# Reordering the head of a fused GroupNorm, CondConv and sign-convolution kernel

## The chip, the cores and the metric

The kernel runs on one core of a Trainium2 chip. The metric is the time on the device in microseconds (us); the median of several runs counts. Engines are named as the profile names them: PE is TensorE, DVE is VectorE, ACT is ScalarE, POOL is GpSimd, SP is SyncE, which here only issues DMAs.

## What is computed

The input is x, 16 images of 128 channels of 32 x 32, in float32. Reference, cut:

```python
def gn(v):    # 32 groups of 4 channels, over the group's channels and pixels
    return (v - mean_g(v)) / sqrt(var_g(v) + 1e-5)

def cond(x, w_route, b_route, w_experts, bn...):
    routing = sigmoid(mean_hw(x) @ w_route.T + b_route)         # 4 experts
    y = conv3x3(x, w_experts)                                   # (B, E, 128, 32, 32)
    out = einsum("beohw,be->bohw", y, routing)
    return silu(out * inv + (bn_beta - bn_mean * inv))

x = x + cond(gn(x))
x = x + conv3x3(gn(x), sign(W))
```

The sum over experts is done on the weights: for each image the four expert kernels are mixed by its routing into one 3 x 3 kernel.

## The kernel before

Channels lie on the 128 partitions, one image is 1,024 columns. Each image goes through the same steps:

- the statistics of the input (`nm` mean, `var` variance), by DVE with `bn_stats` for image 0 (`half_stats`, `aggregate`), by ACT with two passes over the image for the others (`mean_in`, `var_in`);
- a chain of small operations, numbered c. PE sums the means over each group (`group_means`), ACT squares the deviations (`deviations`), PE sums the variances (`group_vars`), DVE takes them over (`variance`), POOL raises them to -0.5 (`power`, `rstd`), DVE makes `nbias`, `zr` and `pooled` (`biases`, `pool_routes`), PE sums `pooled` over the channels (`route_logits`), ACT makes `route` (`routing`). All results of PE in it lie in one PSUM bank, `ps`;
- ACT normalises the image into `xn` (`normalise`) and weighs the first expert into `U` (`mix`), DVE adds the other three (`mix(i, e)`; row by row for image 0, `mix_row`);
- the first convolution. Image 0 is done directly, in six parts (`direct_part(0, n, half)`: three kernel rows n, two halves), from `xn` and `U` into bank pair `pd`. Images 1 to 15 use Winograd's form along the rows: DVE transforms `xn` into `V` (`transform_sums`, `transform`) and `U` into `UM` (`even_rows`, `kernel_rows`), PE multiplies (`minus_points`, `plus_points`, `end_points`, into `pb`, `pa`, `pe_`), ACT copies `pb` (`copy_minus`), DVE inverts into `y` (`inverse_inner`, `inverse_outer`);
- ACT applies silu, and the result is added to the image in `X` (`residual`, by DVE for images 0, 14 and 15, by a DMA with addition from POOL's queue for the others);
- the statistics of the sum go with chain c = i + 3 (`mean_mid`, `var_mid`), which also serves the input of image i + 3. ACT normalises the sum to `hi` (float16) and `hn`, DVE takes their difference `lo` (`low_part`), PE convolves `hi` and `lo` with the signs of W (`sign_half`, line 425) into the bank pair `pc`, ACT copies it out (`evacuate`) and a DMA adds it to the stored sum.

Each engine has an order written out by hand, and counting semaphores tie them. In pass t of the main loop PE does the points of image t, then the sign convolution of image t - 1; DVE mixes for image t + 1, inverts image t, makes `lo` of t - 1 and transforms image t + 2. Ahead of the loop is the head, which the change is about. There PE does `WARM[0]` = 9 products of ones, after a wait for the parameters (`prm_loaded`), then chain 0 with `route_logits(0)`, `WARM[1]` = 8 more, then the six direct parts with chains 1 and 2 strung between them (lines 456 to 476). A float32 product is two instructions in the trace. The groups before DVE's main loop are at lines 881 to 913, ACT's at 626 to 651, the loads of SP at 272 to 284. SP issues the two halves of image 0, the parameters, weight row G1, image 1, weight rows G0 and G2, images 2 and 3, and the signs' weights.

Of the kernel before, what the change touches and what calls it, by code (L numbers as in the profile page):

```python
# [45 lines left out]
WARM = (9, 8)  # L46
# [4 lines left out]
def build(nc, x, w_experts, w_sign, params, out):  # L51
# [6 lines left out]
    with ExitStack() as ctx:  # L58
# [45 lines left out]
        halves = sb("halves", [C, 2, 6])  # L104
        agg = {i: sb(f"agg{i}", [C, 2]) for i in (0, B - 1)}
# [21 lines left out]
        gnm = ps[:, 0:2 * CHAINS].rearrange("p (c k) -> p c k", k=2)  # L127
        gvar = ps[:, 64:64 + 2 * CHAINS].rearrange("p (c k) -> p c k", k=2)
        logits = ps[:, 128:128 + E * B].rearrange("p (i e) -> p i e", e=E)
# [91 lines left out]

        def dma_added_before(i):

            return sum(1 for j in range(i % 2, i, 2) if j not in DVE_RESIDUAL)
# [40 lines left out]
        def _(sp):  # L265
# [72 lines left out]
        def _(pe):  # L338
# [6 lines left out]
            def group_means(c):  # L345
# [9 lines left out]
                mm_(gnm[:, c, a:b], gmat[:], nm[:, c, a:b], start=True, stop=True).then_inc(gnm_ready, 1)  # L355

            def group_vars(c):
# [6 lines left out]
                mm_(gvar[:, c, a:b], gmat[:], var[:, c, a:b], start=True, stop=False)  # L364
                mm_(gvar[:, c, a:b], gmat_hw[:], dev2[:, c, a:b], start=False, stop=True).then_inc(gvar_ready, 1)  # L365

            def route_logits(i):
                pe.wait_ge(pooled_ready, i + 1)
                mm_(logits[:, i, :], ones[:], pooled[:, i, :], start=True, stop=True).then_inc(logits_ready, 1)  # L369
# [87 lines left out]
            pe.wait_ge(prm_loaded, 16)  # L457
# [50 lines left out]
        def _(act):  # L508
# [28 lines left out]
            def deviations(c):  # L537
                a, b = cols(c)
                act.wait_ge(gnm_ready, c + 1)
                for k in range(a, b):  # L540
                    activation(dev2[:, c, k:k + 1], gnm[:, c, k:k + 1], ACT.Square, bias=nm[:, c, k:k + 1],
                               scale=-1.0).then_inc(dev2_ready, 1)

            def normalise(i):
# [5 lines left out]
                activation(xn[i % 2][:, 1:1 + H, :], img(i).rearrange("p (h w) -> p h w", h=H), ACT.Identity,  # L550
# [128 lines left out]
        def _(dve):  # L679
# [234 lines left out]
            for t in range(1, B + 1):  # L914

                c = t + LAG - 1
                if t > 1:
                    mix(t + 1, 1)
# [63 lines left out]
```

## Time and profile before

| | |
|---|---|
| median of 3 runs | 303.5 us (302.35 to 303.65) |
| profiled execution, its own time | 302.17 us |
| its span, first to last instruction | 300.3 us |
| mean granted clock of PE | 0.983 |
| PE busy | 278.8 us (93%) |
| DVE busy | 254.9 us (85%) |
| ACT busy | 188.8 us (63%) |
| POOL busy | 42.8 us (14%) |

The profile is of one execution. Its time is 1.9 us more than its span, for what lies before the first and after the last instruction, and 1.3 us less than the median. A timeline row gives the start, the duration (of a group: from its first start to its last end), the engine and line, what is written from what, the count, and in brackets the idle time before it with what ended it. Ends overlap with the next start by up to some 0.1 us, so costs are best read from start to start.

### The profile page before, as it was taken

The numbers are of one execution on the slowest core, as the hardware profiler recorded it, in microseconds if no ns is written. First come the engines' busy times: TensorE is split into PE (matmuls) and PEld (weight loads), VectorE is DVE, ScalarE is ACT, GpSimd is POOL, SyncE is SP. The second block draws the span as 40 slices with busy tenths as digits, with TensorE's granted clock in tenths as the row PEclk, the third lists the DMA queues.
The fourth block names the chain that finished last, engine by engine and source line by source line (L and its number), as shares of the span: only waits on it lengthen the run. The fifth ranks groups of instructions, "written<-read, shape, count | busy, mean of one in ns | idle before, by whom it ended". The sixth has DMA issues, their size and how long they took to land.

```text
span 300.3 us, 3929 instructions
## 1 busy us (share of the span) xinstructions
PE 278.8 (93%) x1350; PEld 193.8 (65%) x1350; DVE 254.9 (85%) x487; ACT 188.8 (63%) x300; POOL 42.8 (14%) x56
## 2 busy tenths in 40 slices
PE   3799692699999999999999999999999999999896
PEld 3754381367685859585867677676858595858454
DVE  3238989789999999999999999999999999960932
ACT  1446370768778687769595968687786874644230
POOL 2001200102121212121211202021212121201000
PEclk9999979699999999999999999999999999999999
DMA  7999410054544453626263544545453436230411
GB/s 244 396 383 323 168 72 0 1 140 72 140 70 113 70 100 93 119 80 120 83 104 105 82 131 70 142 70 141 71 123 67 91 86 127 79 63 0 70 72 70
DMA packets 10963, 34.14 MB, mean 114 GB/s; under 512 B 1216, under 2 KB 3008, under 8 KB 10944
## 3 DMA queue, kind: packets, MB, share of 16 engines
q0 software_dynamic: 3888, 14.16, 28.0%
q1 hardware_dynamic: 7056, 19.74, 17.4%
q8 instruction: 11, 0.18, 0.2%
q14 instruction: 8, 0.07, 0.1%
HBM read 11.34 MB, written 15.73 MB: 90 GB/s over the span
## 4 chain that ended last, share of the span: by engine, by line
PE 83%; DVE 11%; ACT 2%; issue 1%; DMA 1%; POOL 0%; SPq 0%; DVEq 0%; ACTq 0%
PE pc L425 40%; PE pa L390 12%; PE pb L390 12%; PE pe_ L390 11%; DVE U L764 3%; PE pd L343 3%; PE pd L380 2%; PE ps L365 1%; DMA prm<-params 1%; PE ps L364 1%; DVE e_rows L796 1%; PE ps L355 1%; PE ps L369 1%; PE pb L425 1%; DVE U L754 1%
## 5 line engine op out<-in xcount | busy, mean ns | idle before, releaser
L425 PE MATMUL pc<-lo,ws 128*128 128x496 f16 (+5 forms) x288 | 64.7, 372 | 0.0
L764 DVE SCALAR_TENSOR_TENSOR U<-we,route,U 128x1152 f32<-128x1152 f32 x45 | 63.8, 1417 | 1.0
L425 PE MATMUL pc<-hi,ws 128*128 128x496 f16 (+5 forms) x288 | 63.9, 377 | 0.4 <-ACT hi L610 0.4
L425 PEld LDWEIGHTS pc<-hi,ws 128*128 128x128 f16 x288 | 28.5, 102 | 30.9 <-issue 2.2
L425 PEld LDWEIGHTS pc<-lo,ws 128*128 128x128 f16 x288 | 28.2, 102 | 28.2 <-DVE lo L872 0.3
L390 PE MATMUL pa<-V,UM 128*128 128x256 f32 (+1 forms) x180 | 42.0, 383 | 0.0
L390 PE MATMUL pb<-V,UM 128*128 128x256 f32 (+1 forms) x180 | 42.0, 384 | 0.0
L305 POOL TENSOR_TENSOR rstd<-ve,nhalf 128x2 f32<-128x2 f32 (+1 forms) x19 | 17.2, 905 | 168.1 <-DVE ve L728 168.1
L390 PE MATMUL pe_<-V,U 128*128 128x256 f32 (+1 forms) x180 | 40.6, 375 | 0.0
L390 PEld LDWEIGHTS pb<-V,UM 128*128 128x128 f32 x180 | 34.9, 194 | 5.2
L390 PEld LDWEIGHTS pe_<-V,U 128*128 128x128 f32 x180 | 34.1, 190 | 3.8
L390 PEld LDWEIGHTS pa<-V,UM 128*128 128x128 f32 x180 | 33.3, 192 | 3.3
L610 ACT ACTIVATE hi<-X,nbias,rstd 128x1024 f16<-128x1024 f32 (+2 forms) x17 | 20.1, 1190 | 17.9 <-DVE nbias L734 17.9
L534 ACT ACTIVATE junk_mid<-X,nm 128x1024 f32<-128x1024 f32 x15 | 17.2, 1148 | 17.6 <-DMA X<-y 16.7
L550 ACT ACTIVATE xn<-X,nbias,rstd 128x1024 f32<-128x1024 f32 x16 | 19.7, 1229 | 11.3 <-DVE nbias L734 11.3
L584 ACT ACTIVATE minus<-pb 128x512 f32<-128x512 f32 x15 | 8.9, 596 | 27.7 <-PE pb L390 27.7
L872 DVE TENSOR_TENSOR lo<-hn,hi 128x1024 f16<-128x1024 f32 x16 | 19.5, 1217 | 3.2 <-ACT hn L617 3.2
L595 ACT ACTIVATE y<-y,bn_shift,bn_tiles 128x1024 f32<-128x1024 f32 x14 | 17.4, 1240 | 6.3 <-DVE y L847 6.3
L309 POOL DMA_DIRECT2D X<-y x13 | 11.5, 884 | 65.8 <-ACT y L595 65.8
L728 DVE TENSOR_SCALAR ve<-ps 128x2 f32<-128x2 f32 (+1 forms) x19 | 2.9, 153 | 20.6 <-PE ps L365 20.6
L617 ACT ACTIVATE hn<-X,nbias,rstd 128x1024 f32<-128x1024 f32 x16 | 19.6, 1227 | 0.0
L796 DVE SCALAR_TENSOR_TENSOR e_rows<-xn 128x1024 f32<-128x1024 f32 x15 | 18.3, 1220 | 0.9 <-ACT xn L550 0.9
(85 smaller groups left out, 389.0 us busy)
## 6 DMA issues: line engine op xcount, KB each, us to landing
X<-x SPq DMA_DIRECT2D x15, 512.0 KB, 5.2
out<-X SPq DMA_DIRECT2D x14, 512.0 KB, 2.6
out<-ev POOLq DMA_DIRECT2D x14, 512.0 KB, 5.4
X<-y POOLq DMA_DIRECT2D x13, 512.0 KB, 4.5
we<-w_experts SPq DMA_DIRECT2D x3, 768.0 KB, 7.3
out<-X SPq DMA_DIRECT2D x3, 256.0 KB, 2.0
ws_raw<-w_sign SPq DMA_DIRECT2D x1, 576.0 KB, 10.8
X<-x SPq DMA_DIRECT2D x2, 256.0 KB, 2.8
```

The costliest lines, as they stand in the source:

```text
L305: g.tensor_tensor(rstd[:, c, a:b], ve[:, c, a:b], nhalf[:, a:b], ALU.pow).then_inc(rstd_ready, 1)
L309: g.dma_start(img(i), flat3(y[i % 2][:]), accum_op=ALU.add).then_inc(added[i % 2], 16)
L390: mm = mm_(bank[:, :, j, c0:c1], weights[:, kx * C:(kx + 1) * C], V[t % 2][:, :, k, c0 + kx - 1:c1 + kx - 1], start=(n == 0), stop=(n == K ...
L425: mm = mm_(rows[:, r0 - first // W:r1 - first // W, c0:c1], ws[:, tap * C:(tap + 1) * C], (hi, lo)[part][i % 2][:, r0 + ky - 1:r1 + ky - 1 ...
L534: activation(junk["mid"][:], img(i), ACT.Square, bias=nm[:, c, MID:MID + 1], scale=1.0 / ROOT_HW, accum_out=var[:, c, MID:MID + 1]).then_i ...
L550: activation(xn[i % 2][:, 1:1 + H, :], img(i).rearrange("p (h w) -> p h w", h=H), ACT.Identity, bias=nbias[:, i, IN:IN + 1], scale=rstd[:, ...
L595: activation(flat3(y[i % 2][:]), flat3(y[i % 2][:]), ACT.Silu, bias=bn_shift[:, 0:1], scale=bn_tiles[:, 0:1], accum_out=ysum[:, i:i + 1]). ...
L610: activation(hi[i % 2][:, first:last, :], img(i).rearrange("p (h w) -> p h w", h=H)[:, first:last, :], ACT.Identity, bias=nbias[:, c, MID: ...
L617: activation(hn[:], img(i), ACT.Identity, bias=nbias[:, c, MID:MID + 1], scale=rstd[:, c, MID:MID + 1]).then_inc(hn_ready, 1)
L764: v.scalar_tensor_tensor(out=flat(U[i % 2][:]), in0=flat(we[:, e, :, :]), scalar=route[:, i, e:e + 1], in1=flat(U[i % 2][:]), op0=ALU.mult ...
L796: v.scalar_tensor_tensor(out=flat3(e_rows[:]), in0=flat(xn[i % 2][:, 0:H, :]), scalar=-4.0, in1=flat(xn[i % 2][:, 2:2 + H, :]), op0=ALU.mu ...
L872: v.tensor_tensor(flat(lo[i % 2][:]), hn[:], flat(hi[i % 2][:]), ALU.subtract).then_inc(lo_ready, 1)
```

## The change

- Loads: image 1 is issued right behind the parameters, ahead of weight row G1.
- PE: the warm products don't wait for the parameters any more; 4 instead of 8 products after the first chains. Chains 0 and 1 run side by side before the direct parts, chain 2 between them. Chains 1 and 2 write to the banks of `pc` (`small_bank`), so that `group_means` of 1 and 2 waits for nothing of the chain before.
- DVE: the statistics of image 1 by `bn_stats`, ahead of `variance(0)`; chain 1 ahead of the mixing of image 0; in the head `variance(2)`, `biases(2)`, `pool_routes(2)` one step later or earlier among the mixes of image 1, and `residual(0)` behind the transform of image 2.
- DVE, pass 1: `variance(3)`, the inverse of image 1 and the biases first, then the mixes 2 and 3 of image 2 with `low_part(0)` between them, then its even and kernel rows. The two first operations of `inverse_inner` are a function of their own, `inverse_sums`.
- ACT: image 0 is normalised in two parts (17 and 15 rows), the first weighted row G1 between them; the first product of PE waits for the first part alone. `sign_weights`, `routing(2)` and `var_in(3)` go ahead of `silu(0)`, `copy_minus(1)` ahead of `var_mid(0)`.
- Passes from 2 on keep their order.

```diff
-WARM = (9, 8)
+WARM = (9, 4)
...
+        def small_bank(c):
+            return pc[:, c - 1, :] if c in (1, 2) else ps[:]
...
             sp.dma_start(prm[:], params).then_inc(prm_loaded, 16)
+            load(1)
             load_row(G1, 1)
-            load(1)
...
-                wait(pe, nbias_ready, c)
-                wait(pe, zr_ready, min(c, B))
-                wait(pe, th_ready, min(c, B))
+                if c > 2:
+                    last = 1 if c == 3 else c
+                    pe.wait_ge(nbias_ready, last)
+                    pe.wait_ge(zr_ready, min(last, B))
+                    pe.wait_ge(th_ready, min(last, B))
...
-                pe.wait_ge(xn_ready, i + 1)
+                pe.wait_ge(xn_ready, 1 if i == n == half == 0 else i + 2)
...
             pe.wait_ge(zeroed, 2)
-            pe.wait_ge(prm_loaded, 16)
             warm(WARM[0])
             pe.wait_ge(gmat_ready, 2)
             group_means(0)
             group_vars(0)
+            group_means(1)
+            group_vars(1)
             route_logits(0)
+            route_logits(1)
             warm(WARM[1])
-
             direct_part(0, 0, 0)
-            group_means(1)
             direct_part(0, 0, 1)
-            group_vars(1)
             direct_part(0, 1, 0)
-            route_logits(1)
+            group_means(2)
             direct_part(0, 1, 1)
-            group_means(2)
+            group_vars(2)
             direct_part(0, 2, 0)
-            group_vars(2)
+            route_logits(2)
             direct_part(0, 2, 1)
-            route_logits(2)
...
             act.wait_ge(nm_in_ready, 1)
             deviations(0)
-            normalise(0)
+            act.wait_ge(nm_in_ready, 2)
+            deviations(1)
+            act.wait_ge(nbias_ready, 1)
+            normalise_rows(0, 0, H // 2 + 1)
             routing(0)
-            mix(0)
-            mean_in(1)
-            var_in(1)
-            deviations(1)
+            mix_first_row(0, G1)
+            normalise_rows(0, H // 2 + 1, H)
+            mix_first_row(0, G0)
+            mix_first_row(0, G2)
+            routing(1)
+            normalise(1)
+            mix(1)
             mean_in(2)
-            normalise(1)
-            routing(1)
-            mix(1)
             var_in(2)
             deviations(2)
             mean_in(3)
+            sign_weights()
             normalise(2)
-            sign_weights()
+            routing(2)
+            var_in(3)
             silu(0)
             mean_mid(0)
-            routing(2)
             mix(2)
-            var_mid(0)
-            var_in(3)
             for t in range(1, B):
-                if t > 1:
+                if t == 1:
+                    copy_minus(t)
                     var_mid(t - 1)
                     deviations(t + LAG - 1)
-                copy_minus(t)
-                if t == 1:
+                else:
+                    var_mid(t - 1)
                     deviations(t + LAG - 1)
+                    copy_minus(t)
...
             aggregate(0, 0, IN, nm_in_ready, var_in_ready)
             parameters()
+            dve.wait_ge(x_loaded[1], 16)
+            half_stats(1, 0)
+            half_stats(1, 1)
+            aggregate(1, 1, IN, nm_in_ready, var_in_ready)
             variance(0)
             dve.wait_ge(route_prm_ready, 2)
             biases(0)
             pool_routes(0)
+            variance(1)
+            biases(1)
+            pool_routes(1)
             batch_norm()
             mix_row(0, 0)
             mix_row(0, 1)
-            variance(1)
             mix_row(0, 2)
-            biases(1)
-            pool_routes(1)
             transform_sums(1)
             transform(1)
             mix(1, 1)
+            variance(2)
             mix(1, 2)
-            variance(2)
+            biases(2)
+            pool_routes(2)
             mix(1, 3)
             even_rows(1)
-            biases(2)
             kernel_rows(1, -1)
-            pool_routes(2)
             kernel_rows(1, 1)
-            residual(0)
             transform_sums(2)
             transform(2)
+            residual(0)
             mix(2, 1)
...
                 if t == 1:
+                    variance(c)
+                    inverse_sums(t)
+                    biases(c)
+                    pool_routes(c)
+                    inverse_inner(t)
+                    inverse_outer(t)
+                    mix(t + 1, 2)
+                    low_part(t - 1)
+                    mix(t + 1, 3)
+                    even_rows(t + 1)
                     kernel_rows(t + 1, -1)
                     kernel_rows(t + 1, 1)
-                    inverse_inner(t)
-                    variance(c)
-                    inverse_outer(t)
-                    biases(c)
-                    pool_routes(c)
```

## Rows read from the trace of the kernel before

**Rows 1.** Waits over the whole run: engine, line, waited for, total, times, longest us.

```profile
PE ps L369 <- DVE pooled L744: 12.0, 3, 7.8
...
DVE ve L728 <- PE ps L365: 20.6, 5, 7.2
```

**Rows 2.** Busy time of each engine in one steady pass, with clock and DMA.

```profile
72.80:88.75 15.95, 15.95 (x83) 11.26 (x82) 15.67 (x30) 11.99 (x19) 2.74 (x3) 1.00 0.47 99
```

**Rows 3.** Timeline of PE: start, duration, line, operation, count, idle before.

```profile
4.58 4.18 PE L343 MATMUL pd<-ones 128*128 128x128 f32 x18 [4.58 <-DMA prm<-params]
8.55 0.42 PE L355 MATMUL ps<-nm,gmat 128*128 128x1 f32 x2
...
16.03 3.30 PE L380 MATMUL pd<-xn,U 128*128 128x512 f32 x6
...
19.30 2.77 PE L380 MATMUL pd<-xn,U 128*128 128x512 f32 x6
...
30.90 2.61 PE L380 MATMUL pd<-xn,U 128*128 128x480 f32 x6
...
36.45 4.14 PE L390 MATMUL pb<-V,UM 128*128 128x256 f32 x12
...
55.58 5.25 PE L425 MATMUL pc<-hi,ws 128*128 128x512 f16 x18 [0.39 <-ACT hi L610]
...
72.80 3.97 PE L425 MATMUL pc<-hi,ws 128*128 128x512 f16 x18
```

**Rows 4.** Timeline of DVE, same columns.

```profile
3.44 1.40 DVE L714 BATCH_NORM_STATS2 halves<-X 128x6 f32<-128x512 f32 x2 [1.25 <-DMA X<-x]
...
10.53 0.16 DVE L728 TENSOR_SCALAR ve<-ps 128x1 f32<-128x1 f32 x1 [5.00 <-PE ps L365]
...
11.75 0.22 DVE L744 SCALAR_TENSOR_TENSOR pooled<-wroute,zr,bshare 128x4 f32<-128x4 f32 x1
...
13.84 3.76 DVE L754 SCALAR_TENSOR_TENSOR U<-we,route,U 128x384 f32<-128x384 f32 x6 [1.41 <-ACT U L564]
...
29.50 2.87 DVE L764 SCALAR_TENSOR_TENSOR U<-we,route,U 128x1152 f32<-128x1152 f32 x2
...
73.61 1.22 DVE L872 TENSOR_TENSOR lo<-hn,hi 128x1024 f16<-128x1024 f32 x1
```

**Rows 5.** Waits of DVE between 13.8 and 73.7 us.

```profile
DVE ve L728 <- PE ps L365: 5.7, 2, 4.8
DVE lo L872 <- ACT hn L617: 2.1, 1, 2.1
DVE X L853 <- ACT y L591: 1.4, 1, 1.4
...
DVE e_rows L796 <- ACT xn L550: 0.9, 1, 0.9
```

**Rows 6.** Third large load; then landing times of X and of the weight rows.

```profile
2.12 0.43 SPq L270 DMA_DIRECT2D we<-w_experts  x1
...
DMA to landing us min/median/max: 2.7/4.8/9.9
...
DMA to landing us min/median/max: 5.0/7.3/9.0
```

**Rows 7.** Busy time and clock, one microsecond after the pause of PE.

```profile
38.00:39.00 1.00, 1.00 (x4) 0.82 (x3) 0.49 (x1) 0.94 (x5) 0.00 (x0) 0.50 0.00 0
```

**Rows 8.** POOL: the power of chain 2, and all powers of the page.

```profile
32.52 1.71 POOL L305 TENSOR_TENSOR rstd<-ve,nhalf 128x1 f32<-128x1 f32 x1 [8.98 <-DVE ve L728]
...
L305 POOL TENSOR_TENSOR rstd<-ve,nhalf 128x2 f32<-128x2 f32 (+1 forms) x19 | 17.2, 905 | 168.1 <-DVE ve L728 168.1
```

**Rows 9.** Timeline of ScalarE (ACT), same columns as Rows 3.

```profile
34.99 1.24 ACT L550 ACTIVATE xn<-X,nbias,rstd 128x1024 f32<-128x1024 f32 x1 [5.31 <-DVE nbias L734]
...
43.03 0.39 ACT L541 ACTIVATE dev<-ps,nm 128x1 f32<-128x1 f32 x2
...
83.29 0.60 ACT L584 ACTIVATE minus<-pb 128x512 f32<-128x512 f32 x1 [1.84 <-PE pb L390]
```

More of the change, by code:

```diff
@@ L220, in cols, with gnm, gvar, logits @@
             return (IN if c < LAG else MID), (2 if c < B else 1)
+        def small_bank(c):
+            return pc[:, c - 1, :] if c in (1, 2) else ps[:]
+        def gnm(c, a, b):
+            return small_bank(c)[:, 2 * c + a:2 * c + b]
+        def gvar(c, a, b):
+            return small_bank(c)[:, 64 + 2 * c + a:64 + 2 * c + b]
+        def logits(c):
+            return small_bank(c)[:, 128 + E * c:128 + E * (c + 1)]
         def dma_added_before(i):
@@ L350, in group_means @@
                     pe.wait_ge(nm_mid_ready, c - LAG + 1)
[L352 to L355 removed]
+                if c > 2:
[3 more added lines that the diff above has]
+                    pe.wait_ge(th_ready, min(last, B))
+                mm_(gnm(c, a, b), gmat[:], nm[:, c, a:b], start=True, stop=True).then_inc(gnm_ready, 1)
             def group_vars(c):
@@ L363, in group_vars @@
                 pe.wait_ge(dev2_ready, dev2s(c))
-                mm_(gvar[:, c, a:b], gmat[:], var[:, c, a:b], start=True, stop=False)
-                mm_(gvar[:, c, a:b], gmat_hw[:], dev2[:, c, a:b], start=False, stop=True).then_inc(gvar_ready, 1)
+                mm_(gvar(c, a, b), gmat[:], var[:, c, a:b], start=True, stop=False)
+                mm_(gvar(c, a, b), gmat_hw[:], dev2[:, c, a:b], start=False, stop=True).then_inc(gvar_ready, 1)
             def route_logits(i):
                 pe.wait_ge(pooled_ready, i + 1)
-                mm_(logits[:, i, :], ones[:], pooled[:, i, :], start=True, stop=True).then_inc(logits_ready, 1)
+                mm_(logits(i), ones[:], pooled[:, i, :], start=True, stop=True).then_inc(logits_ready, 1)
             def direct_part(i, n, half):
                 slot, ky = ((G1, 1), (G0, 0), (G2, 2))[n]
-                pe.wait_ge(xn_ready, i + 1)
+                pe.wait_ge(xn_ready, 1 if i == n == half == 0 else i + 2)
                 pe.wait_ge(mixed, mixes_before(i) + (E - 1) * (n + 1))
@@ L549, in normalise, with normalise_rows @@
                     act.wait_ge(direct_ready, 2 * (i - 1))
-                activation(xn[i % 2][:, 1:1 + H, :], img(i).rearrange("p (h w) -> p h w", h=H), ACT.Identity,
+                normalise_rows(i, 0, H)
+            def normalise_rows(i, first, last):
+                activation(xn[i % 2][:, 1 + first:1 + last, :],
+                           img(i).rearrange("p (h w) -> p h w", h=H)[:, first:last, :], ACT.Identity,
                            bias=nbias[:, i, IN:IN + 1], scale=rstd[:, i, IN:IN + 1]).then_inc(xn_ready, 1)
@@ L560, in mix @@
                 act.wait_ge(route_ready, i + 1)
-                if i < ND:
-                    for g in (G1, G0, G2):
-                        act.wait_ge(we_loaded[g], 16)
-                        activation(U[i % 2][:, g, :], we[:, 0, g, :], ACT.Copy,
-                                   scale=route[:, i, 0:1]).then_inc(mix_first, 1)
-                    return
                 if i - 2 >= ND:
@@ L574, in mix, with mix_first_row @@
                            scale=route[:, i, 0:1]).then_inc(mix_first, 1)
+            def mix_first_row(i, g):
+                act.wait_ge(route_ready, i + 1)
+                act.wait_ge(we_loaded[g], 16)
+                activation(U[i % 2][:, g, :], we[:, 0, g, :], ACT.Copy, scale=route[:, i, 0:1]).then_inc(mix_first, 1)
             def sign_weights():
@@ L935, in _ @@
                     kernel_rows(t + 1, 1)
+                    inverse_sums(t)
                     inverse_inner(t)
                     inverse_outer(t)
-                elif t == B - 1:
-                    variance(c)
-                    biases(c)
-                    inverse_inner(t)
-                    inverse_outer(t)
-                if t < B:
                     low_part(t - 1)
```

44 lines of the change are left out of this document (21 added, 23 removed).

## The prediction, made before the changed kernel was run

> **What bounds the kernel now.** I read first the waits of TensorE (PE) over the whole run, then busy time in stretches of the steady part, then the timelines of the head, engine by engine. The waits say where PE is not the bound: 12.0 us behind `pooled`, in three waits, the longest 7.8 us [rows 1]; all three lie before 55 us. From the first sign convolution at 55.58 on, PE is busy to the end but for 1.2 us in the tail. In the stretches one image costs PE 15.95 us of 15.95, at full clock, and VectorE (DVE) 15.67 us of the same 15.95 [rows 2]. The DVE rest of 0.28 is in small gaps, so DVE's own pass is hardly shorter than PE's. Two consequences. Whatever time PE's steady part starts earlier, the end comes earlier by the same, if DVE comes along. And DVE hardly catches up: what it is late at the second image it is late until the last images, where it has nothing left to mix (a single wait of 7.2 us there [rows 1]). The question is therefore where DVE and PE stand when image 1 is reached: DVE's `low_part(1)`, before at 73.61 [rows 4], and PE's convolution of image 1, before at 72.80 [rows 3].
>
> **The new start, step by step.** PE's warm products no longer wait for the parameters. Before they began at 4.58 and the group means of image 0 stood behind them until 8.55 [rows 3]. Now they begin at about 1.0 (the ones are filled by then), last the same 3.97, and end at 5.0, before the statistics of image 0, which DVE has at 5.3. So the means go at 5.35, and `variance(0)` could be fed 10.53 - 8.55 = 1.98 later, at 7.3 [rows 3, 4].
>
> It isn't, because DVE now has the statistics of image 1 ahead of it. Image 1 now takes the place of the first weight row, issued at 2.12. Loads of X land 2.7 to 9.9 us after issue, median 4.8; the weight row in that place is the quickest of the three, 5.0 us [rows 6]. Image 1 is 256 KB smaller, 0.65 us at the 400 GB/s of this stretch, so I take 4.3 us: it lands at 6.4 (ends 4.8 and 12.0). Its statistics last as image 0's, which began at 3.44 [rows 4] and ended at 5.3, 1.85 us: until 8.3. Then `variance(0)` at 8.3 instead of 10.53, `pooled(0)` 1.44 later as before, at 9.75. Chain 1 runs in banks of its own: means at 8.35, `variance(1)` 1.98 later at 10.35, `pooled(1)` ready 1.44 later at 11.8, and `batch_norm` ends at 12.3. ScalarE has the first image's route at 11.3 and, with half an image normalised instead of a whole one, the first weighted row at 11.9; the weights, now behind image 1, land at 8.5 at the latest by the sum above and are hidden. So DVE starts mixing at 12.3 instead of 13.84 [rows 4]: gain 1.5. Three mixes of 0.63 (3.76 for six) end at 14.2. PE has its second logits until 12.3 and then 8 warm passes instead of 16, 1.8 us at the 0.22 of the first 18, so it ends at 14.1 and hides behind the mixes. The first product starts at s = 14.3 instead of 16.03: gain 1.7.
>
> **The clock.** The first direct part takes 3.30 us where its twins take 2.77 [rows 3]: so half rate held until about 17, though the clock column doesn't record it. After the later pause the column does: 0.50 at 38 to 39 [rows 7]. Nothing in the change makes PE busier before 14.3 than it was, so I let it rise at the same 17: 2.7 us at half rate, of which 1.35 is lost, where 0.5 was. c = 1.3, with the ends 0.3 (it rises as early after the first activity as the earlier start allows) and 3.0.
>
> **Image 0 and the fill.** The wait of PE on DVE goes over to DVE waiting on PE. DVE does the three mixed rows, the transform of image 1 and its first mix without a stop. That is the time from 13.84 to 30.95, the middle of the two mixes at 29.50, less the idle 4.8 and 0.9 and the 0.5 of chain 1 that is now done before [rows 4, 5]: 10.8 us, so until 23.1. The wait of 4.8 is gone, but `variance(2)` stands next, and PE reaches the variances of image 2 only after four direct parts. These are s + c + 10.9 = 26.5 (14.87 from 16.03 to 30.90, less 0.5 for the clock, one part of 2.77 and small ones [rows 3]): DVE idles 3.4 us here. This is the largest new wait; behind it are the mixes 2 and 3 of image 1 and with them PE's first minus points.
>
> The `rstd` of chain 2 took 1.71 us beside mixes of 1.42 us [rows 8]; with one mix between it and its use, DVE waits 0.45 more. By the Trainium skill ("SBUF — State Buffer", section "SBUF: two separate sides") the port pair that VectorE and GpSimd share is locked for a whole instruction, so the power would wait out the mix and then take its own time; the row agrees, and by that rule nothing more is lost at `variance(3)`, where the operations behind it read one operand from PSUM.
>
> From `variance(2)` at 26.5: mix 1.5, wait and biases 0.9, mix 1.45, even rows 0.95, kernel rows 1.9: the last kernel row for PE's minus points is ready at 32.3 and PE ends the direct parts at s + c + 16.0 = 31.6. So the minus points start at 31.9 instead of 36.45 [rows 3], without the pause of 2.7 us and, I take it, without the fall of the clock that cost 1.4 of their 4.14 us. DVE goes on with the transform of image 2, the residual and a mix until 39.5. ScalarE has from the end of the direct parts on what it had between 34.99 and 43.4 [rows 9], less the signs of the weights (1.05, now in an idle piece) and plus 0.4 for the residual it waits for: 8.0 us, until 39.7. So PE has the variances of image 3 at 40.2 and `variance(3)` is at 40.25: DVE idles 0.75. Before it waited 2.1 for `hn` and 0.9 for `variance(4)` [rows 5]; neither is left, for ScalarE gets its biases at 41.7, `hi(0)` is there at 42.9, and the first convolution starts at 43.0 instead of 55.58, 12.5 us earlier.
>
> That is not the gain, for DVE still owes its work. From 13.84 to 73.61 it had 59.77 us, of which 5.7 + 2.1 + 1.4 + 0.9 = 10.1 were idle [rows 5]: 49.6 of work, 49.1 without chain 1. The reordering in pass 1 (inverse before the mixes of image 2) changes none of it. So `low_part(1)` is at 12.3 + 49.1 + 3.4 + 0.45 + 0.75 = 66.0; adding the same operations one by one I get 65.7. I take 65.8: DVE gains 7.8.
>
> **What PE gains over DVE.** In the steady part PE may stand earlier against DVE than it did. Three links hold it. `lo` is ready 1.15 + 0.1 after `low_part` starts, and is wanted 3.8 after the convolution starts (18 products, 3.97 with their overlap [rows 3]): 73.61 + 1.25 against 72.80 + 3.8, room 1.75. `hi` comes one ScalarE pass behind `nbias`, long before `low_part`, and has more room. The residual's DMA and the statistics of the sum end 1.84 before the minus points that ScalarE then waits for [rows 9]: room 1.65. The smallest decides, so PE's convolution of image 1 is at 65.8 - 0.81 - 1.65 = 63.3; by the `hi` link alone it could start at 62.4. Before it PE idles 2.6 us with only the logits in it, about the pause (36.45 less 33.5, the end of the direct parts) after which the clock fell, and with a fall it counts as 63.8. I take 63.5, gain 9.3. From there on it is the old order at 15.95 a pass, and the tail has room for DVE's 1.5 us of lag.
>
> **The sum.** 72.8 - 63.5 = 9.3 us. The profiled run lasted 302.17 us, with a span of 300.3; it would become 292.9. It is 1.3 us under the median of the three runs, 303.5, so the forecast for a median is 294.2.
>
> **Rivals.** First, nothing over DVE: the DMA of the residual or the fall of the clock takes the 1.5 us by which PE moves up, gain 7.8, 295.7 us; against it, the 1.84 us of room in a steady pass. Chance 0.2. Second, the clock stays at half rate for most of the direct parts (c = 3), or image 1 lands a microsecond or two later than I take: each late microsecond goes through `variance(0)` to everything; gain 6 to 7.5, 296 to 297.5. For it: the head loads fully use the DMA. Chance 0.15. Third, the change doesn't do what it says: the first chain and the pauses of PE in pass 1 stay, because ScalarE's queue (silu, minus copy, then the residual statistics) is late, and only the 1.7 of the start and a clock fall of 1.4 are saved: 300.4. ScalarE's 8.0 us beside DVE's 7.9 speak against. Chance 0.06. Fourth, slower: DVE is the bound of every pass once PE has moved up, and its pass is longer than 15.95. The place is `nbias` behind `rstd`: where the power waits out a mix it took 1.71 where the mean of all is 0.9 [rows 8], 0.8 more a pass, over 13 passes 10.4 us against the 9.3 gained: 304.6. It decides from 0.7 us a pass. Against it, in passes after the first the operations beside the power are the same short ones. Chance 0.03. Fifth, better: the clock rises early (c = 0.3) or image 1 lands 2.7 after issue, the quickest of all, so that the chain of image 0 runs by its own inputs, at 7.3: 1.0 each, gain 10.3 to 11, 292.8. Chance 0.14. My forecast, 293.3 to 295.2, has 0.42.
>
> **How the numbers follow.** The low end takes in the fifth case and a median that lies only 0.3 over the profiled run, as two runs of before allow: 291.3. The high end takes in the first two cases: 298.0. What a measurement of this kernel can tell from no change is about 0.5%, 1.5 us. Only the third and fourth case and mishaps reach there: faster 0.93, same 0.04, slower 0.03.
>
> **What would show it.** Right: PE's first product at 14.3, DVE idle about 3.4 us before `variance(2)` near 26.5 and under 1 us before `variance(3)` near 40, minus points of image 1 at 31.9, the first convolution near 43, PE idle about 2.6 us before the convolution of image 1 at 62.4 to 64, passes of 15.95 after it. Wrong: a pass of more than 16.0 (fourth), a wait of PE for `dev` or `lo` in every pass (first), a first product later than 15 or direct parts of 5 us (second), or a pause over 4 us before the first convolution (third).

## The result, and the profile after

| | before | after |
|---|---|---|
| median | 303.28 us (302.35 to 303.65, 4 runs) | 293.07 us (292.71 to 293.47, 4 runs) |
| profiled execution, its own time | 302.17 us | 292.85 us |
| its span | 300.3 us | 291.0 us |
| PE busy | 278.8 us (93%) | 276.5 us (95%) |
| DVE busy | 254.9 us (85%) | 255.8 us (88%) |
| ACT busy | 188.8 us (63%) | 185.6 us (64%) |

The ratio of the times is 0.967, with the interval 0.965 to 0.970. The median before is of four runs here, the profiled one among them. The span is shorter by 300.3 - 291.0 = 9.3 us. Of these, PE's idle time gives 7.0 (21.5 before, 14.5 after). PE's busy time fell by 2.3, for the minus points of image 1 and the first sign convolution no longer run at the lower clock, as the rows below show.

The timeline of PE after, in the columns of [rows 3]:

```profile
1.03 4.21 PE L353 MATMUL pd<-ones 128*128 128x128 f32 x18 [1.03 <-POOL ones L327]
5.43 0.56 PE L367 MATMUL ps<-nm,gmat 128*128 128x1 f32 x2 [0.19 <-DVE nm L738]
...
14.00 8.72 PE L392 MATMUL pd<-xn,U 128*128 128x512 f32 x18
...
28.60 2.61 PE L392 MATMUL pd<-xn,U 128*128 128x480 f32 x6
31.31 2.78 PE L402 MATMUL pb<-V,UM 128*128 128x256 f32 x12
...
42.68 3.97 PE L437 MATMUL pc<-hi,ws 128*128 128x512 f16 x18
...
61.09 0.39 PE L381 MATMUL ps<-pooled,ones 128*128 128x4 f32 x2 [1.84 <-DVE pooled L761]
61.98 3.98 PE L437 MATMUL pc<-hi,ws 128*128 128x512 f16 x18 [0.51 <-ACT hi L623]
66.36 2.08 PE L437 MATMUL pc<-lo,ws 128*128 128x512 f16 x9 [0.40 <-DVE lo L892]
69.11 0.39 PE L367 MATMUL ps<-nm,gmat 128*128 128x2 f32 x2 [0.66 <-ACT junk_mean L524]
...
79.45 3.97 PE L437 MATMUL pc<-hi,ws 128*128 128x512 f16 x18
```

Against [rows 3], the warm products start at 1.03 instead of 4.58, the first direct product at 14.00 instead of 16.03, the minus points of image 1 at 31.31 instead of 36.45 and at full rate (2.78 us, not 4.14), the first sign convolution at 42.68 instead of 55.58 and at full rate (3.97, not 5.25). Ahead of image 1's convolution PE idles 1.84 + 0.51 us, and there the clock did not fall: 3.98 us. Behind it stand two small waits, 0.40 for `lo` and 0.66 for ACT's `junk_mean`, the image mean. The pass before has one of them, 0.33 for `junk_mean` at 48.88; from 79.45 on the passes are the old ones. Counted back from there, image 1's convolution stands at 79.45 - 15.95 = 63.50, where it was at 72.80: the 9.3 us of the span.

The timeline of DVE after, same columns:

```profile
6.59 1.29 DVE L731 BATCH_NORM_STATS2 halves<-X 128x6 f32<-128x512 f32 x2 [1.04 <-DMA X<-x]
8.29 0.15 DVE L745 TENSOR_SCALAR ve<-ps 128x1 f32<-128x1 f32 x1
...
10.20 0.16 DVE L745 TENSOR_SCALAR ve<-pc 128x1 f32<-128x1 f32 x1 [0.48 <-PE pc L377]
...
11.94 5.60 DVE L771 SCALAR_TENSOR_TENSOR U<-we,route,U 128x384 f32<-128x384 f32 x9
...
25.84 0.16 DVE L745 TENSOR_SCALAR ve<-pc 128x1 f32<-128x1 f32 x1 [3.30 <-PE pc L377]
...
27.76 0.16 DVE L751 SCALAR_TENSOR_TENSOR nbias<-pc,rstd 128x1 f32<-128x1 f32 x1 [0.44 <-POOL rstd L315]
...
39.83 0.16 DVE L745 TENSOR_SCALAR ve<-ps 128x2 f32<-128x2 f32 x1 [1.00 <-PE ps L377]
...
65.10 1.21 DVE L892 TENSOR_TENSOR lo<-hn,hi 128x1024 f16<-128x1024 f32 x1
...
81.03 1.21 DVE L892 TENSOR_TENSOR lo<-hn,hi 128x1024 f16<-128x1024 f32 x1
```

Image 1 is in at 6.59. The new wait of DVE is 3.30 us before `variance(2)`, and it is the largest one left before the tail. `low_part(1)` is at 65.10 instead of 73.61 [rows 4], so DVE gained 8.5 us, and the next follows 15.93 later.

Busy time after, in a steady pass and in two microseconds of the head (columns: stretch, its length, busy time of PE, weight loads, DVE, ACT, POOL with counts, granted clock, DMA share, GB/s):

```profile
15.00:16.00 1.00, 1.00 (x3) 0.48 (x2) 0.96 (x3) 1.00 (x2) 0.00 (x0) 0.50 1.03 413
16.00:17.00 1.00, 1.00 (x4) 0.53 (x3) 0.93 (x3) 1.00 (x2) 0.00 (x0) 0.92 1.02 401
...
78.95:94.90 15.95, 15.95 (x82) 11.21 (x81) 15.67 (x30) 11.89 (x21) 2.66 (x3) 1.00 0.48 100
```

The steady pass is that of [rows 2]: 15.95 us, DVE busy for 15.67. In the head the clock was at the lower of its two levels, 1.2 GHz, until about 16.2, while PE already worked on the direct parts.

### The profile page after: what moved, and what is told of

Read it like the earlier page. It is cut to its first block, busy times and chain, and to the rows that moved or that the text cites. A ratio compares the mean times of both kernels' runs of the same rounds, so it can differ in the third digit from the quotient of the medians.

```text
span 291.0 us, 3911 instructions
## 1 busy us (share of the span) xinstructions
PE 276.5 (95%) x1342; PEld 190.6 (66%) x1342; DVE 255.8 (88%) x492; ACT 185.6 (64%) x297; POOL 41.8 (14%) x56
## 3 DMA queue, kind: packets, MB, share of 16 engines
q1 hardware_dynamic: 7056, 19.74, 18.2%
## 4 chain that ended last, share of the span: by engine, by line
PE 78%; DVE 9%; issue 6%; ACT 3%; DMA 2%; POOL 1%; SPq 0%; ACTq 0%; DVEq 0%; POOLq 0%
PE pc L437 36%; PE pa L402 12%; PE pb L402 11%; PE pe_ L402 10%; PE pd L392 4%; DMA X<-x 2%; PE ps L377 1%; POOL rstd L315 1%; ACT y L608 1%; DVE halves L731 1%; PE ps L367 1%; DVE sums L841 1%; PE ps L376 1%; PE pd L353 1%; PE pb L437 1%
## 5 line engine op out<-in xcount | busy, mean ns | idle before, releaser
L437 PE MATMUL pc<-hi,ws 128*128 128x496 f16 (+5 forms) x288 | 62.6, 372 | 0.7 <-ACT hi L623 0.5
L402 PE MATMUL pb<-V,UM 128*128 128x256 f32 (+1 forms) x180 | 40.6, 375 | 0.1
L402 PEld LDWEIGHTS pb<-V,UM 128*128 128x128 f32 x180 | 34.2, 190 | 5.7 <-issue 0.8
L563 ACT ACTIVATE xn<-X,nbias,rstd 128x1024 f32<-128x1024 f32 (+2 forms) x17 | 20.0, 1178 | 6.4 <-PE pd L392 6.1
L581 ACT ACTIVATE U<-we,route 128x1152 f32<-128x1152 f32 x15 | 18.6, 1240 | 0.0
L813 DVE SCALAR_TENSOR_TENSOR e_rows<-xn 128x1024 f32<-128x1024 f32 x15 | 18.2, 1216 | 0.0
```

The source lines that it names most:

```text
L402: mm = mm_(bank[:, :, j, c0:c1], weights[:, kx * C:(kx + 1) * C], V[t % 2][:, :, k, c0 + kx - 1:c1 + kx - 1], start=(n == 0), stop=(n == K ...
L437: mm = mm_(rows[:, r0 - first // W:r1 - first // W, c0:c1], ws[:, tap * C:(tap + 1) * C], (hi, lo)[part][i % 2][:, r0 + ky - 1:r1 + ky - 1 ...
L563: activation(xn[i % 2][:, 1 + first:1 + last, :], img(i).rearrange("p (h w) -> p h w", h=H)[:, first:last, :], ACT.Identity, bias=nbias[:, ...
L581: activation(flat(U[i % 2][:]), flat(we[:, 0, :, :]), ACT.Copy, scale=route[:, i, 0:1]).then_inc(mix_first, 1)
L813: v.scalar_tensor_tensor(out=flat3(e_rows[:]), in0=flat(xn[i % 2][:, 0:H, :]), scalar=-4.0, in1=flat(xn[i % 2][:, 2:2 + H, :]), op0=ALU.mu ...
```

## The experiments

All kernels compute the full result. In a diff "after" is the changed kernel. Spans and starts are of the profiled execution; times are medians, against the kernel before on the same chip.

**1 and 2. How much of the gain is the new order of DVE's pass 1?** Taken out of the changed kernel:

```diff
                 if t == 1:
-                    variance(c) ... inverse_outer(t)
-                    mix(t + 1, 2)
-                    low_part(t - 1)
-                    mix(t + 1, 3) ... kernel_rows(t + 1, 1)
+                    mix(t + 1, 2) ... kernel_rows(t + 1, 1)
+                    inverse_sums(t); inverse_inner(t)
+                    variance(c)
+                    inverse_outer(t)
+                    biases(c); pool_routes(c)
+                    low_part(t - 1)
```

> The changed kernel, with pass 1 of VectorE in the old order (mixes 2 and 3, even and kernel rows of image 2 ahead of the inverse of image 1). Theory: TensorE must start its convolution of image 0 early enough to be held by VectorE and not by its own work. Here it waits again some 6 us for the logits and hi, starts the convolution near 49.5 instead of 42.7, at half rate, and its convolution of image 1 counts from about 66.8 instead of 63.5: 3.3 us more than the changed kernel, about 296.4. low_part(1) of VectorE moves by 1 to 2 us only. Rival (VectorE alone sets the end, the order within pass 1 is free): within 1.3 us of the changed kernel's 293.1, as low_part(1) moves.

Measured: 297.59 us, ratio 0.983 (0.979 to 0.987), span 295.1, 4.1 more than after. PE's timeline:

```profile
48.70 0.59 PE L381 MATMUL ps<-pooled,ones 128*128 128x4 f32 x2 [6.25 <-DVE pooled L761]
49.68 5.97 PE L437 MATMUL pc<-hi,ws 128*128 128x512 f16 x18 [0.39 <-ACT hi L623]
...
67.63 3.97 PE L437 MATMUL pc<-hi,ws 128*128 128x512 f16 x18
```

With the old order PE stands 6.25 us behind `pooled`, and the first convolution, 7.0 us later than in after, runs at the lower clock until about 53.8 (5.97 us against 3.97). The fall cost 2.0 where I had 1.3. Of these 7.0 + 2.0 more than half is given back, because image 1's convolution no longer waits for anything: it follows at 67.63, 4.1 behind the 63.50 of after. DVE's timeline:

```profile
50.70 1.23 DVE L892 TENSOR_TENSOR lo<-hn,hi 128x1024 f16<-128x1024 f32 x1 [2.05 <-ACT hn L630]
...
62.51 0.16 DVE L745 TENSOR_SCALAR ve<-ps 128x2 f32<-128x2 f32 x1 [1.61 <-PE ps L377]
...
68.44 1.21 DVE L892 TENSOR_TENSOR lo<-hn,hi 128x1024 f16<-128x1024 f32 x1
```

I had expected `low_part(1)` to move by 1 to 2 us only. It moves by 3.3, to 68.44, for DVE now waits for `hn` and, one pass later, for the variances that PE delivers late. So the late PE holds DVE too, and of the 4.1 us, 3.3 are DVE's and 0.8 are the lead of PE over DVE, which is the old 0.81 again (68.44 - 67.63).

The other way round, the same new order put into the kernel before, with its old head:

> The kernel before, with pass 1 of VectorE in the new order, and nothing else. Theory: VectorE loses its two idle pieces behind pass 1 (2.06 and 0.88 us), so low_part(1) is at about 70.7 instead of 73.6 and TensorE's convolution of image 1 stands 1.6 us ahead of it, at 69.1: 3.7 us faster than before, 299.6. Rival (the 12 us of TensorE's waits are the gain): the wait of 7.8 us goes, and 8 to 9 us are gained, 295.

Measured: 296.98 us, ratio 0.980 (0.977 to 0.984), span 294.7, 5.6 less than before. PE's and then DVE's timeline:

```profile
15.32 2.76 PE L380 MATMUL pd<-xn,U 128*128 128x512 f32 x6
...
65.54 5.67 PE L425 MATMUL pc<-hi,ws 128*128 128x512 f16 x18 [0.51 <-ACT hi L610]
...
83.19 3.97 PE L425 MATMUL pc<-hi,ws 128*128 128x512 f16 x18
```

```profile
68.65 1.21 DVE L875 TENSOR_TENSOR lo<-hn,hi 128x1024 f16<-128x1024 f32 x1
```

The gain lies between my theory (299.6) and the rival (295), and the trace splits it. The head, whose code is the old one, ran 1.27 us earlier: the direct parts start at 15.32, not at 16.03, and the first lasts 2.76, not 3.30 [rows 3]. Both differences are PE's clock. In chain 0 the products of `group_vars` lasted 0.35 and 0.36 us, where before they lasted 0.56 each, so DVE had `variance(0)` at 9.94 instead of 10.53; and the rise before the direct parts came at about 15.1, ahead of the first one. From the end of DVE's head (38.38, before 39.65) to `low_part(1)` it takes 30.27 us where it took 33.96: 3.7 for the new order, of which the two waits that I had named are 2.9. PE moves up against DVE by another 0.6 (83.19 - 15.95 = 67.24, 1.41 ahead of `low_part`, where it was 0.81 ahead). So the order is worth 3.7 + 0.6 = 4.3 us added alone and 4.1 taken out, and the rest of the change 9.3 - 4.1 = 5.2. The 1.27 of the head is no gain of the edit. Whether it lies in the other three runs of this kernel too (296.7 to 297.6) no trace shows, nor why the clock rose earlier.

**3. The wait of 3.30 before `variance(2)`.** The means and variances of image 2 one direct part earlier on PE:

```diff
-            direct_part(0, 1, 0)
             group_means(2)
-            direct_part(0, 1, 1)
+            direct_part(0, 1, 0)
             group_vars(2)
+            direct_part(0, 1, 1)
```

> The changed kernel, with the group means and variances of image 2 one direct part earlier in TensorE's order. VectorE's wait of 3.3 us before variance(2) falls to about 0.6. Theory: nothing is gained, within 0.4 us of 293.1, since the transform of image 2 then waits for ScalarE to normalise image 2 into the buffer that the direct parts read until 31.2; the wait comes back there, some 2.7 us long. Rival (the wait of VectorE is on the path): 2.5 us faster, 290.6.

Measured: 293.52 us, ratio 0.969 (0.966 to 0.972), span 291.7. DVE's waits between 11 and 75 us:

```profile
DVE e_rows L813 <- ACT xn L563: 2.3, 1, 2.3
DVE ve L745 <- PE pc L377: 1.5, 1, 1.5
```

The wait shrinks from 3.3 to 1.5, and a new one of 2.3 for image 2's `xn` stands behind it. `xn` has two buffers; ACT can't write image 2 into that of image 0 before PE's last direct part. So this wait can't be removed where it shows: the same idle time sits behind the buffer. The span of 291.7 is no loss either: the clock rose late in this profile (at about 17.8), and the repeat of after in experiment 9, where it rose at 17.6, has the same 291.7.

**4. The same with a third buffer.**

```diff
-        xn = [sb(f"xn{p}", [C, PH, W]) for p in range(2)]
+        xn = [sb(f"xn{p}", [C, PH, W]) for p in range(3)]
+        def xb(i):
+            return xn[2 if i == 2 else i % 2]
...
-                elif i - 2 >= 0:
-                    act.wait_ge(direct_ready, 2 * (i - 1))
```

> The changed kernel, with a third buffer for the normalised image 2 and the group variances of image 2 one direct part earlier. Theory (the buffer that the direct parts read is what took back the gain of the earlier variances): ScalarE normalises image 2 near 25, VectorE has no wait of 2.3 us before its transform, variance(3) comes 2.6 us earlier than 39.8 and low_part(1) 2.6 us earlier than 65.1: 2.6 us faster than the changed kernel, 290.5, span 288.4. Rival (the end of the direct parts holds the statistics of the sum of image 0 through silu, so VectorE waits just as long before variance(3)): no gain, span 291.

Measured: 290.74 us, ratio 0.961 (0.956 to 0.966), span 288.7, 2.3 less than after. DVE's and then PE's timeline:

```profile
37.47 0.16 DVE L746 TENSOR_SCALAR ve<-ps 128x2 f32<-128x2 f32 x1 [1.01 <-PE ps L380]
...
62.75 1.22 DVE L893 TENSOR_TENSOR lo<-hn,hi 128x1024 f16<-128x1024 f32 x1
```

```profile
23.41 5.29 PE L395 MATMUL pd<-xn,U 128*128 128x512 f32 x12
...
77.12 3.97 PE L440 MATMUL pc<-hi,ws 128*128 128x512 f16 x18
```

`variance(3)` comes 2.36 earlier, `low_part(1)` 2.35, PE's next pass 2.33. A microsecond that DVE gains before image 1 reaches the end whole. That is the main reading of the prediction, and here it is shown by a change of its own. (The row of twelve direct products serves experiment 6.)

**5. What holds PE to DVE?** The 0.66 us for `junk_mean` was in none of my links. ACT makes the input mean of a later image behind silu and the mix; put before the mix:

```diff
                 if t < B - 1:
                     mean_mid(t)
+                if t + LAG < B:
+                    mean_in(t + LAG)
                 if t + 2 < B:
                     mix(t + 2)
                 if t + LAG < B:
-                    mean_in(t + LAG)
                     var_in(t + LAG)
```

> The changed kernel, with mean_in(t+3) ahead of mix(t+2) on ScalarE, so that the input mean of the next chain is there 1.2 us earlier. Theory: this mean is the link that holds TensorE to VectorE in the steady part (its wait in pass 2 was 0.85 us with the hand-over), TensorE moves up by 0.8 us: 292.3, span 290.2. Rival (VectorE's own lateness or the residual's DMA holds TensorE): no change, span 291.0 within 0.2.

Measured: span 290.3, 0.7 less than after, as expected. The times don't show it: the median is 294.31 (ratio 0.970, 0.965 to 0.975), and while the profiled run took 292.2, the other three took 293.9 to 294.8, more than any of the four of after (292.7 to 293.5). What made them longer no trace shows. So this experiment shows the link in a timeline, not a faster kernel. PE's timeline:

```profile
61.92 3.98 PE L437 MATMUL pc<-hi,ws 128*128 128x512 f16 x18 [0.51 <-ACT hi L623]
...
78.75 3.97 PE L437 MATMUL pc<-hi,ws 128*128 128x512 f16 x18
```

Image 1's convolution starts as in after (61.92 against 61.98), the next one 0.70 earlier. ACT's row in after shows the link in its own time:

```profile
67.92 1.04 ACT L524 ACTIVATE junk_mean<-X 128x1024 f32<-128x1024 f32 x1
68.87 0.19 ACT L524 ACTIVATION_READ_ACCUMULATOR junk_mean<-X 128x1 f32 x1
```

The sum is read at 69.06, and PE's `group_means` goes at 69.11.

**6. Is the clock's rise set by what PE does in the pauses before the direct parts?** Two warm products in each of two pauses, and, apart from that, eight instead of four behind the chains:

```diff
             group_vars(0)
+            warm(2)
             group_means(1)
             group_vars(1)
             route_logits(0)
+            warm(2)
             route_logits(1)
```

> The changed kernel, with two products of ones in each of TensorE's two pauses of over 1 us before the direct parts (before the means of image 1 and before its logits). Theory of the first look at the runs: the clock rises 1 to 3.5 us after the first direct product and the moment differs from run to run (15.0 to 17.6 us in the runs so far); activity in the pauses lets it rise before 14.5, so that no direct product runs at half rate, and the end comes up to 1.0 us earlier than the changed kernel's span of 291.0: 290.0. Rival (the moment does not hang on such short pauses): first direct product at 14.0 to 14.3, rise at 15 to 17.6 as before, span 290.5 to 291.8.

```diff
-WARM = (9, 4)
+WARM = (9, 8)
```

> The changed kernel, with 8 instead of 4 warm products ahead of the first direct part. They last 1.8 us, so the first direct product goes at 15.8 instead of 14.0. Theory: they replace direct products at half rate, of which the runs had 0.9 to 1.9 us of loss, by others at half rate; 0.2 to 1.2 us slower, 0.6 in the middle, span 291.6. Rival (they are lost whole): 1.8 us slower, span 292.8.

Measured: 293.59 us for the first (ratio 0.968, 0.964 to 0.973, span 292.1), 294.25 for the second (0.972, 0.968 to 0.975, span 292.9). The first 18 direct products, of the one and of the other:

```profile
14.26 9.60 PE L392 MATMUL pd<-xn,U 128*128 128x512 f32 x18
```

```profile
16.33 8.32 PE L392 MATMUL pd<-xn,U 128*128 128x512 f32 x18
```

At full rate these 18 take 7.65 us: a row of twelve of 512 columns takes 5.29 (experiment 4), the six of 480 columns 2.61, less the 0.25 by which such rows overlap (2 x 2.77 - 5.29). So the loss was 1.95 with products in the pauses, where after lost 1.07 in its first profile and 1.80 in the repeat of experiment 9; the rise came at 18.2. That profile speaks against my theory that they bring the rise forward, and the median shows no gain. With eight products the direct parts start 2.3 later and lose 0.67; the rise came at about 17.8. Of the 2.3, the products make 1.6. The other 0.7 was there before them: image 1 came at 7.04 instead of 6.59, and the small products of chain 1 ran at the lower clock. So the span, 1.9 above the first profile of after and 1.2 above the second, makes the price look too high. By the medians, 294.25 against the 293.77 of after on the same chip, the two are not told apart: four products are not shown to be better than eight.

**7. Waiting for the parameters again, and image 1 behind the weight row G1:**

```diff
             pe.wait_ge(zeroed, 2)
+            pe.wait_ge(prm_loaded, 16)
             warm(WARM[0])
```

> The changed kernel, with TensorE's wait for the parameters put back ahead of the warm products. Theory: the products run from 4.6 to 8.6, the chains follow later, VectorE starts to mix at 14.2 instead of 11.94 and the first direct product goes at 16.3 instead of 14.0; of these 2.3 us some 0.8 come back because fewer direct products run at half rate: 1.5 us slower than the changed kernel, 294.6, span 292.5. Rival (the load and statistics of image 1 hold the start, the wait is hidden): within 0.4 of the changed kernel.

```diff
             sp.dma_start(prm[:], params).then_inc(prm_loaded, 16)
-            load(1)
             load_row(G1, 1)
+            load(1)
```

> The changed kernel, with image 1 issued behind the first weight row again. Theory: image 1 lands 1.3 us later than 6.5, variance(0) stands behind its statistics and everything up to the first direct product moves by 1.3, half of it returned by the clock: 0.7 us slower than the changed kernel, 293.8, span 291.7. Rival (the DMAs interleave, the place in the order is nothing): image 1 lands within 0.4 us of 6.5 and the span stays at 291.0.

Measured: 295.41 us (ratio 0.975, 0.971 to 0.980), span 293.2, for the wait; 295.74 us (0.977, 0.972 to 0.981), span 294.7, for the load. PE with the wait:

```profile
15.50 9.41 PE L392 MATMUL pd<-xn,U 128*128 128x512 f32 x18
```

DVE and then PE with the late load:

```profile
9.02 1.29 DVE L731 BATCH_NORM_STATS2 halves<-X 128x6 f32<-128x512 f32 x2 [3.43 <-DMA X<-x]
```

```profile
16.70 9.71 PE L392 MATMUL pd<-xn,U 128*128 128x512 f32 x18
```

The wait moves the direct parts by 1.5, and 0.7 more is lost to the clock: 2.2, the rise of the span. By the ratios the wait is apart from the first measurement of after (0.965 to 0.970) but not quite from the repeat (0.967 to 0.974). The load moves image 1's statistics from 6.59 to 9.02 and the direct parts by 2.7; 1.0 more went to the clock, so the span rose by 3.7. I had expected that a later start finds the clock nearer to its rise and gets part back; it got nothing. This profile was the slowest of its kernel's four runs: by the medians the load order is worth 2.0 to 2.7 us (295.74 against the 293.77 and 293.07 of after, measured on other occasions), by the span 3.7; the wait by the medians 1.6 to 2.3. The pieces can't be added up: both work through the start of the direct parts.

**8. Is DVE as close a bound as PE in the steady part?** One more DVE operation of 256 columns in each transform of images 4 to 15, whose output nothing reads:

```diff
+                if 4 <= i:
+                    wait(dve, extra_ready, i - 4)
+                    v.tensor_tensor(extra[:], e_rows[:, :, 2, :], e_rows[:, :, 1, :], ALU.add) \
+                     .then_inc(extra_ready, 1)
```

> The changed kernel, with one more operation of VectorE of 256 columns in each transform of images 4 to 15, 0.34 us each, which nothing reads. Theory: in the steady part VectorE's pass is 15.93 against TensorE's 15.95, so nothing hides it: 12 times 0.32, about 3.8 us more, span 294.8, and TensorE waits in nearly every pass. Rival (VectorE has slack against TensorE, as its busy time of 15.67 says): 0.28 of each are hidden, 0.7 us more in all.

Measured: 296.62 us, ratio 0.979 (0.975 to 0.983), span 293.6. One steady pass in busy times, and the waits of the weight loads between 70 and 260 us (engine, line, waited for, total, times, longest):

```profile
95.08:111.36 16.28, 16.22 (x84) 11.19 (x82) 16.00 (x31) 11.88 (x20) 2.67 (x3) 1.00 0.46 97
```

```profile
PEld ps L369 <- ACT junk_mean L526: 5.5, 10, 0.6
```

The pass went from 15.95 to 16.28: the whole operation (0.42 us alone, 0.33 to the next one's start) came on top, in ten passes. So the 0.28 us by which DVE's busy time is below the pass is no room; it is hand-overs. The row also shows how such a pass hides: PE counts 16.22 of 16.28 as busy, and only the weight loads show the wait, 0.55 a pass, again for ACT's mean. That is the path from DVE back to PE: DVE's inverse, silu, mix, `junk_mean`, `group_means`. I had reckoned with all twelve operations, 3.8 us. Ten times 0.33 is 3.3; the span rose by 2.6 because this run's head was 0.65 earlier.

**9. The third buffer and the early mean together**, with the changed kernel again beside it on the same chip:

> The changed kernel, with the third buffer and the early variances (e_third_xn) and with mean_in(t+3) ahead of mix(t+2) (e_mean_first). Theory: the two act on different things, the first on where VectorE stands, the second on how far TensorE may stand ahead of it, so their gains add: 2.3 + 0.7 = 3.0 us less than the changed kernel's span of 291.0, 288.0, give or take 0.5 for the moment at which the clock rises. Rival (TensorE's own chain is the bound once VectorE has moved up): 288.7 as with the third buffer alone.

> The changed kernel once more, beside e_both on the same chip. 293.1 us, span 290.5 to 291.8 by the moment at which the clock rises.

Measured: 290.20 us (289.7 to 291.3, six runs), ratio 0.959 (0.956 to 0.962), span 288.3, against 293.77 us (293.2 to 294.6, six runs), ratio 0.970 (0.967 to 0.974), span 291.7. That is 3.6 us, 1.2%, below the changed kernel on the same chip. PE in the first and in the second:

```profile
59.09 5.67 PE L440 MATMUL pc<-hi,ws 128*128 128x512 f16 x18 [0.51 <-ACT hi L624]
...
76.73 3.97 PE L440 MATMUL pc<-hi,ws 128*128 128x512 f16 x18
```

```profile
62.72 5.29 PE L437 MATMUL pc<-hi,ws 128*128 128x512 f16 x18 [0.43 <-ACT hi L623]
...
80.19 3.97 PE L437 MATMUL pc<-hi,ws 128*128 128x512 f16 x18
```

In both the clock fell in the pause before image 1's convolution (5.67 and 5.29 us, not 3.97). In the repeat of after it cost nothing: the next pass counts back to 80.19 - 15.95 = 64.24, 1.59 before that run's `low_part` at 65.83, the same lead as the 1.60 of the first profile, in which the clock held. The 0.7 us by which its span is longer lie in the head (18 direct products in 9.45 us instead of 8.72). The mean's link sets the time there, and PE's slower products lie under it. With the early mean that cover is gone: PE leads DVE by 1.42 instead of 2.23 as in experiment 5, so the fall took 0.8 back. Against the third buffer alone (ratio 0.961) the two together are not told apart.

## Why the prediction was right, and where it was not

| step | predicted us | measured us |
|---|---|---|
| means of image 0 | 5.35 | 5.43 |
| statistics of image 1 start | 6.4 | 6.59 |
| `variance(0)`, `variance(1)` | 8.3, 10.35 | 8.29, 10.20 |
| DVE starts mixing | 12.3 | 11.94 |
| first direct product | 14.3 | 14.00 |
| lost to the clock there (c) | 1.3 | 1.07 |
| `variance(2)`, idle before it | 26.5, 3.4 | 25.84, 3.30 |
| minus points of image 1 | 31.9 | 31.31 |
| `variance(3)`, idle before it | 40.25, 0.75 | 39.83, 1.00 |
| first sign convolution | 43.0 | 42.68 |
| `low_part(1)` | 65.8 | 65.10 |
| convolution of image 1: starts, counts as | 62.4, 63.5 | 61.98, 63.50 |
| profiled execution | 292.9 | 292.85 |
| median | 294.2 | 293.07 |

**Right.** The two consequences that carried the prediction hold. What DVE gains before image 1 arrives at the end whole: shown by the third buffer (2.35 at DVE, 2.33 at PE, 2.3 in the span). And DVE can't catch up: shown by the added operation, which came on top in full in each of ten passes. The stretch from `variance(2)` to `low_part(1)`, worked out as 39.3 us, took 39.26. The wait for the `rstd` of chain 2 came as costed, 0.44 for 0.45; so by the lock that the Trainium skill describes ("SBUF — State Buffer", section "SBUF: two separate sides"), the trace agrees.

**Two misses that cancelled.** First, DVE gained 8.5, not 7.8. All 0.7 lie before `variance(2)`, which waits for PE: the direct parts start 0.30 earlier and lose 0.23 less to the clock than my 1.3, and the 10.9 us from there to the variances of image 2 were 0.13 less. Second, the step "Three links hold it ... The smallest decides, so PE's convolution of image 1 is at 65.8 - 0.81 - 1.65". There is a fourth link, and it is tighter: DVE's inverse, silu, mix, `mean_in` on ACT, then `group_means` on PE. Before, it had only some 0.9 us of room: in a steady pass of that trace ACT's mean was ready at 77.57 and PE's means went at 78.51.

```profile
77.39 0.18 ACT L514 ACTIVATION_READ_ACCUMULATOR junk_mean<-X 128x1 f32 x1
```

```profile
78.51 0.28 PE L355 MATMUL ps<-nm,gmat 128*128 128x2 f32 x2
```

So PE moved up against DVE by 0.8, not by the 1.5 I took. The profile of experiment 5 shows it: with that link loosened, PE moves up 0.7 more. In the trace before, this link shows no wait, and it is not among the three that I worked out. 8.5 + 0.8 and 7.8 + 1.5 are both 9.3: the exact hit of the span is in part luck.

**The pause before image 1.** I let the convolution count as 63.5 because of a fall of the clock. In the profiled run there was none (pause 1.84 + 0.51, I had 2.6), and in the repeat there was one, with the same lead over `low_part(1)`, 1.59 for 1.60. The figure was right for another reason, the mean's link. Of the rivals, the first (nothing over DVE, for want of room or through the clock) names the right place: half of the expected lead came, though not its gain of 7.8. The second (clock or image 1 late), the third (pauses stay) and the fourth (a pass over 16.0) are each denied by a row above: c = 1.07, the convolution at 42.68, a pass of 15.95. The fifth, better, priced 292.8, near the measured 293.07, but neither of its conditions came: c was not 0.3, and image 1's statistics started at 6.59, not a microsecond and more earlier.

**The median.** 293.07 lies just under the 293.3 to 295.2 to which I gave the largest chance. The whole miss of 1.1 us is the 1.3 I put on for the distance of the median from the profiled run. That distance belongs to the executions, not to the kernel: the changed one lies 0.2 above its profile here and 0.3 in experiment 9, and the medians of before were 302.5 to 303.5 on four occasions. With such a scatter the difference of two profiled runs is no worse a forecast than a difference with the old offset, and the range must hold the offset from zero up.

**The parts.** DVE's order in pass 1 gives 4.1 to 4.3 of the 9.3. The rest of the change gives 5.2, and in it the early start of the warm products (1.6 to 2.3 by itself) and the load order (2.0 to 3.7 by itself) overlap. What the two-part normalisation, the separate banks and ACT's new order give by themselves was not tried. A single profile can be off by a microsecond through the clock in the head, as experiments 2 and 9 show; so these parts are read from starts in the timelines.

## What to carry to other kernels

When two engines have almost the same pass, a gain ahead of the steady part reaches the end only as far as both get it; so compute the new start of each, and then the room of every link between them, those that show no wait included: the tightest was one that had waited for nothing. A wait that sits behind a reused buffer moves, it does not go, until the buffer is doubled. To see whether an engine's small gaps are room, lengthen one of its operations: here 0.28 us of gaps held nothing.

## What the runs showed of the hardware

The moment at which PE's clock rises in the head is not fixed by the program. With the same head it came at 16.2 us in one profile of the changed kernel and at 17.6 in another, in kernels that differ only later at 15.2, 16.0 and 17.8 (experiments 8, 5 and 3), with products added in the pauses at 18.2. The loss on the first direct parts went from nothing (2.76 us in experiment 2) to 2.06 (experiment 7, the late load). A start delayed by a wait did not get closer to the rise: delayed by 1.5 and 2.7 us (experiment 7) it lost 0.7 and 1.0 more. There PE's last pause ended later too, at 13.12 and 14.32 us instead of 11.61. With eight products (experiment 6) the start was 2.3 later, but the last pause ended at 12.33, and the loss was smaller, 0.67. What sets the moment is open: it may hang on the end of the last pause, which no run here varied by itself, and it scatters by over 2 us with the same head. That a few products in the pauses bring it forward, one profile speaks against.

The fall is as little fixed. PE's idle time before image 1's convolution was 1.84 + 0.51 us in one profile of the changed kernel and 1.85 + 0.43 in the other; the clock held in the first (3.98 us for 18 products) and fell in the second (5.29). With 2.27 + 0.51 it held in experiment 5, with 2.28 + 0.51 it fell in experiment 9 (5.67). So a pause of this length is to be priced with and without a fall, 1.3 to 1.7 us here.
